# Nine expert tiles placed between attention's last batch and its routing, with the weight preparation brought forward

## The reference, cut to what matters

```python
def reference(x, ctx, Wq, bq, Wk, bk, Wv, bv, Wr, W1, b1, W2, b2):
    # x (4, 512, 256), ctx (4, 512, 192), all fp32
    q = layernorm(x) @ Wq + bq                 # (4, 512, 256)
    k, v = ctx @ Wk + bk, ctx @ Wv + bv
    x = x + softmax(q @ k.T / sqrt(256)) @ v   # per batch
    z = layernorm(x)
    probs = softmax(z @ Wr.T)                  # 8 experts
    top_v, top_i = top_k(probs, 2)
    top_v = top_v / sum(top_v)
    for e in range(8):                         # W1 (8, 1024, 256), W2 (8, 256, 1024)
        h = gelu(z @ W1[e].T + b1[e])          # exact gelu
        x = x + (h @ W2[e].T + b2[e]) * weight_of_expert(e)
    return x
```

## Time and profile before

| | us |
|---|---|
| median of three runs | 446.9 (446.31 to 447.02) |
| the profiled execution | 444.12 |
| its span, first to last instruction | 442.1 |
| first softmax of batches 0, 1, 2, 3 (ACT) | 37.49, 70.67, 110.05, 151.77 |
| first matmul of tile 0 (PE) | 214.57 |
| POOL's last scatter | 434.06 |
| PE busy over the span | 364.9 (83%) |
| DVE, ACT, POOL busy | 272.9, 234.2, 147.2 |

### The profile page before, as it was taken

How to read it: one execution, slowest core, us unless ns; L and a number is a source line. 1 busy time by engine, 2 the same in 40 slices (tenths; PEclk the granted TensorE clock), 3 DMA queues, 4 the chain that set the end, 5 groups by cost and what they waited for, 6 DMA issues and landing times. The chain is left out here.

```text
span 442.1 us, 10231 instructions
## 1 busy us (share of the span) xinstructions
PE 364.9 (83%) x3384; PEld 289.9 (66%) x3384; DVE 272.9 (62%) x764; ACT 234.2 (53%) x459; POOL 147.2 (33%) x129
## 2 busy tenths in 40 slices
PE   3999989968879795410479999999999999999980
PEld 0344645544646374410469999999999999999970
DVE  1202776687585958688056677776677776677760
ACT  0224668485655665533326656656656666666530
POOL 7300301033536470857003333333333333333331
PEclk9999999999997998655689999999999999999995
DMA  6920025611944292512423335343333333432222
GB/s 214 318 102 0 2 95 192 218 56 49 305 170 131 55 279 101 194 55 84 131 52 49 50 51 51 55 57 51 54 53 56 52 50 49 52 50 38 27 26 24
DMA packets 51794, 40.85 MB, mean 92 GB/s; under 512 B 29440, under 2 KB 47488, under 8 KB 51616
## 3 DMA queue, kind: packets, MB, share of 16 engines
q1 hardware_dynamic: 40416, 26.31, 22.6%
q0 software_dynamic: 7584, 10.57, 13.8%
q10 hardware_dynamic: 3744, 3.31, 2.2%
HBM read 22.41 MB, written 12.66 MB: 79 GB/s over the span
## 5 line engine op out<-in xcount | busy, mean ns | idle before, releaser
L444 POOL DMA_INDIRECT out<-y,meta x39 | 67.7, 1736 | 158.8 <-DVE y L1220 148.2
L855 ACT ACTIVATE g<-s_ps,b_sb,down 128x128 f32<-128x128 f32 x156 | 63.1, 454 | 57.7 <-PE s_ps L650 57.6
L664 PE MATMUL o_ps<-w2h,gh 128*128 x312 | 85.5, 274 | 4.6 <-DVE gl L1191 4.5
L664 PE MATMUL o_ps<-w2l,gh 128*128 x312 | 85.5, 274 | 0.0
L664 PE MATMUL o_ps<-w2h,gl 128*128 x312 | 85.5, 274 | 0.0
L855 ACT ACTIVATE g<-t_ps,b_sb,down 128x128 f32<-128x128 f32 x156 | 63.0, 454 | 40.2 <-PE t_ps L650 40.2
L1189 DVE TENSOR_SCALAR gh<-g,up 128x512 f16<-128x512 f32 x78 | 38.0, 487 | 68.5 <-ACT g L855 54.4
L650 PE MATMUL s_ps<-xs,w1h 128*128 128x128 f16 x624 | 61.4, 222 | 20.5 <-DMA xs<-rows 20.5
L650 PEld LDWEIGHTS s_ps<-xs,w1h 128*128 x624 | 48.6, 99 | 24.0 <-DMA xs<-rows 20.6
L650 PE MATMUL t_ps<-xs,w1h 128*128 128x128 f16 x624 | 60.5, 220 | 0.0
L1191 DVE SCALAR_TENSOR_TENSOR gl<-g,up,gh 128x512 f16<-128x512 f32 x78 | 58.6, 752 | 2.8
(11 more groups left out here) (149 smaller groups left out, 566.8 us busy)
## 6 DMA issues: line engine op xcount, KB each, us to landing
staged<-W1T SPq DMA_DIRECT2D x8, 1024.0 KB, 5.7
staged<-W2T SPq DMA_DIRECT2D x8, 1024.0 KB, 6.0
out<-x_sb ACTq DMA_DIRECT2D x4, 512.0 KB, 7.0
rows<-send POOLq DMA_DIRECT2D x8, 130.0 KB, 7.2
w2l<-ctxT SPq DMA_DIRECT2D x4, 256.0 KB, 4.4
x_sb<-x SPq DMA_DIRECT2D x2, 512.0 KB, 9.0
x_sb<-x ACTq DMA_DIRECT2D x2, 512.0 KB, 5.7
b_sb<-b SPq DMA_DIRECT2D x1, 1024.0 KB, 5.0
```

Of the source, the lines that this page charges most:

```text
L444: pool.indirect_dma_start(out=out, out_offset=bass.IndirectOffsetOnAxis(ap=meta[:, t % XR, 3:4].bitcast(I32), axis=0), in_=y2[:, t % 2, :] ...
L664: i = nc.tensor.matmul(y_ps[t % 2][:, 0:D], l[:, t % 2, m, :], second_weight(w, m, e), start=(m == 0 and k == 0), stop=(m == MC - 1 and k ...
L855: i = nc.scalar.activation(g[:, t % 2, m, :], h_ps[s][:, (m % MQ) * TR:(m % MQ + 1) * TR], ACT.Gelu, bias=b1_sb[:, bass.ds(e, 1), m:m + 1] ...
```

## The change

Nine tiles are taken from batches 0 and 1 alone: full tiles of 128 rows, of which 1024 tokens times 2 give at least nine whatever the routing. Their table (`early_tables`) is worked out by DVE in the last batch, from the row counts after batch 1. SP loads their rows when the sends of batches 0 and 1 are in, and PE starts them right after the last `attend`. The last batch's norm, transpose, logits, routing and sends now stand between these tiles' steps on each engine; three further pieces (`late_tables_1` to `_3`) make the table of the other 30 tiles.

For PE to start there, all 16 units must be prepared by then (`low_ready` 16). So the preparation is regrouped by expert, with one sum and one `scale` for two units: three experts in each of batches 0 and 1 (`SUM_A`, `SUM_B`, `SUM_C`), two in batch 2. The ring still has three slots and the same wait. `XR` goes from 8 to 6, the gated result `y2` has four buffers (`YR`), the gate is multiplied on ACT (`weigh`) and not on DVE, and b2 is loaded after six tiles' rows and not after two. Buffers that were in SBUF only after attention now stand beside it.

```diff
+EARLY = 9
-XR = 8
+XR = 6
+YR = 4
+SUM_A = {0: 0, 1: 3, 2: 6}
+SUM_B = {0: 1, 1: 4}
+SUM_C = {0: 2, 1: 5, 2: 7}
...
@@ sync: the loads of units keep their wait; the contexts move
             for u in range(RING, UNITS):
-                if u % QT == 1 and u // QT + 1 < B:
-                    load_ctx(u // QT + 1)
+                if u == 7:
+                    load_ctx(2)
+                if u == 13:
+                    load_ctx(3)
                 load_unit(u)
...
+            sp.wait_ge(tables_ready, 1)
+            for i in range(2):
+                sp.wait_ge(sent[i], 32 * QT)
+            sp.wait_ge(proj_full, uses["q", B - 1, DC - 1] + 1)
+            for t in range(XR):
                 load_rows(t)
+            sp.wait_ge(low_ready, UNITS - RING + 1)
             sp.dma_start(b2_sb[:], b2.partition_broadcast(P)).then_inc(b2_in, 16)
+            for t in range(XR, EARLY):
+                load_rows(t)
+            sp.wait_ge(tables_ready, 2)
+            for i in range(2):
+                sp.wait_ge(sent[i], 16 * NT)
+            for t in range(EARLY, TILES):
                 load_rows(t)
...
@@ gpsimd: the last batch's sends stand behind the first scatters
             for t in range(TILES):
+                if t == EARLY:
+                    pool.wait_ge(stored, 16 * B)
                 scatter(t)
+                if t < 2:
+                    send_rows(B - 1, t)
...
@@ tensor: in the tile loop
                     hidden(t, m, e_of[t])
+                if (t, m) == (1, 5):
+                    turn_normal(B - 1)
+                if (t, m) == (2, 1):
+                    logits(B - 1)
+                if (t, m) == (3, 2):
+                    ranks(B - 1)
...
@@ scalar: in the loop over batches
+            squares(0)
             for b in range(B):
...
-                if b:
-                    high(u - 1)
-                square(u)
-                if b and b + 1 < B:
+                if last:
+                    high(UNITS - 1)
+                highs(SUM_A, b)
+                if b and not last:
                     load_x(b + 1)
...
+                if b in SUM_B:
+                    squares(SUM_B[b])
+                elif not last:
+                    square(2 * SUM_C[b])
+                if not last:
+                    keys(b + 1)
+                take_turned(b, 3)
+                if not last:
+                    highs(SUM_B, b)
                     turned_rows("xt", b + 1)
+                    if b in SUM_B:
+                        squares(SUM_C[b])
                     values(b + 1)
+                    if b not in SUM_B:
+                        square(2 * SUM_C[b] + 1)
                     queries(b + 1)
                     rows_hi(b)
+                    if b + 1 in SUM_A:
+                        highs(SUM_C, b)
+                        squares(SUM_A[b + 1])
+                    else:
+                        high(2 * SUM_C[b])
...
@@ vector: in the loop over batches
                 row_max(b, 0)
                 if b >= 2:
                     route_places(b - 2)
                 row_max(b, 1)
                 if b:
+                    lows(SUM_C, b - 1)
+                scale(SUM_A, b)
                 row_max(b, 2)
                 invert(b, 0)
                 if b:
                     route_logits(b - 1)
+                ln1_moments(b + 1)
                 residual(b, 0)
                 row_max(b, 3)
                 invert(b, 1)
+                keys(b + 1)
+                ln1_apply(b + 1)
+                lows(SUM_A, b)
                 residual(b, 1)
                 ...
                 values(b + 1, (0, 1))
                 aggregate(1, b, stats2_ready, ln2_var)
+                lows(SUM_B, b)
                 values(b + 1, (2, 3))
                 ...
+                scale(SUM_C, b)
```

More of the change, by code:

```diff
@@ L146, in build, with again_as @@
-        b1q = sa("b1q", [P, E, MC])
-        x_sb = sa("x_sb", [P, 2, QT, D])
+        taken_early = sb("taken_early", [P, E])
+        meta = sb("meta", [P, XR, ROW - D])
+        gates = sb("gates", [P, YR, 3])
+        def again_as(early, late):
+            with ExitStack() as held:
+                first = [sb(*a, scope=held) for a in early]
+            return first, [sb(*a) for a in late]
+        (wq_sb, wk_sb, wv_sb), (xs,) = again_as(
+            [("wq_sb", [P, DC, D]), ("wk_sb", [P, 2, D]), ("wv_sb", [P, 2, D])],
+            [("xs", [P, XR, 2, DC, TR], F16)])
@@ new lines, in _ @@
+            n_late = TILES - EARLY
+            late = slice(EARLY, TILES)
+            by_expert = late_space[:, 0:6 * E].rearrange("p (k e) -> p k e", e=E)
+            by_tile = late_space[:, 6 * E:6 * E + 7 * n_late].rearrange("p (k t) -> p k t", t=n_late)
+            below = late_space[:, LK:LK + E * (N // TR)].rearrange("p (e t) -> p e t", t=N // TR)
+            tile_expert = late_space_2[:, 0:2 * n_late * E].rearrange("p (k t e) -> p k t e", k=2, e=E)
+            count, rest, tiles, last, first, shift = (by_expert[:, k, :] for k in range(6))
@@ new lines, in _, with per_tile, per_expert, late_tables_1 @@
+            ended, mine, less_tile, first_tile, offset, start, region = (by_tile[:, k, :] for k in range(7))
+            product, belongs = tile_expert[:, 0], tile_expert[:, 1]
+            def per_tile(a):
+                return a.unsqueeze(2).to_broadcast([P, n_late, E])
+            def per_expert(a):
+                return a.unsqueeze(1).to_broadcast([P, n_late, E])
+            def late_tables_1():
+                link(nc.vector.tensor_tensor(count, nextrow[:, B, :], base[:], ALU.subtract))
+                link(nc.vector.scalar_tensor_tensor(out=rest, in0=taken_early[:], scalar=-float(TR), in1=count,
+                                                    op0=ALU.mult, op1=ALU.add))
+                link(nc.vector.tensor_tensor(below, rest.unsqueeze(2).to_broadcast([P, E, N // TR]),
+                                             steps[:].unsqueeze(1).to_broadcast([P, E, N // TR]), ALU.is_gt))
+                link(nc.vector.tensor_reduce(tiles, below, AX.X, ALU.add))
+                link(nc.vector.tensor_tensor_scan(last, tiles, none[:], 0.0, ALU.add, ALU.add))
+                link(nc.vector.tensor_tensor(first, last, tiles, ALU.subtract))
+                link(nc.vector.tensor_tensor(shift, first, taken_early[:], ALU.subtract))
@@ L1058, in _, with lows @@
+            def lows(hook, b):
+                if b in hook:
+                    low(2 * hook[b])
+                    low(2 * hook[b] + 1)
             ln1_moments(0)
@@ L1064, in _ @@
             queries(0)
[L1065 to L1066 removed]
+            for b in range(B - 1):
                 row_max(b, 0)
@@ L1122, in _ @@
-            route_first(B - 1)
-            route_second(B - 1)
-            route_gates(B - 1)
-            route_places(B - 1)
-            low(UNITS - 3)
-            low(UNITS - 2)
-            scale(UNITS - 1)
-            dve.wait_ge(gate_ready, B)
-            def per_tile(a):
-                return a.unsqueeze(2).to_broadcast([P, TILES, E])
-            def per_expert(a):
-                return a.unsqueeze(1).to_broadcast([P, TILES, E])
-            count, tiles, last, first = (by_expert[:, k, :] for k in range(4))
@@ L1140, in _ @@
-            ended, mine, less_tile, first_tile, offset, start, region = (by_tile[:, k, :] for k in range(7))
-            product, belongs = tile_expert[:, 0], tile_expert[:, 1]
-            link(nc.vector.tensor_tensor(count, nextrow[:, B, :], base[:], ALU.subtract))
-            link(nc.vector.tensor_tensor(below, count.unsqueeze(2).to_broadcast([P, E, N // TR]),
-                                         steps[:].unsqueeze(1).to_broadcast([P, E, N // TR]), ALU.is_gt))
-            link(nc.vector.tensor_reduce(tiles, below, AX.X, ALU.add))
```

478 lines of the change are left out of this document (256 added, 222 removed).

## The result

After: median **466.41 us** (463.52 to 469.22, four runs). Before, in the same comparison: 446.61 us (441.12 to 447.02, four runs). The ratio is 1.0473 with a 95% interval of 1.0357 to 1.0588: slower, by 4.7%. The forecast was 468 us. The profiled execution took 464.15 us with a span of 462.3, where the sum had 463.0.

A forecast was written before the change was run, and what follows sets the result against it. PE bounds the tiles, not the 39.4 us stretch ahead that the change fills; longer attention puts tile 0 at 230.6, plus tiles 219.5 and tail 12.9 gives 463.0, plus 4.8 gives 467.8, said as 468 us; range 450 to 487.

The forecast's parts named there:

- the sum: Whole kernel: tile 0 at 230.6, tiles 219.5, tail 12.9 give a span of 463.0 us; 4.8 more gives 467.8.
- The ring: Attention, batches 0 and 1: six second squares wait for low, then load, then square, 9.9 us each; 51 us added.
- The three steps between: Attention, first softmaxes of batches 1, 2, 3: 27.3 us later, 30.1 us more, then 6.0 us less.
- The first rival: Attention: ring waits don't add up, only ACT's added 9.8 us counts; tile 0 near 187, 424 us; chance 0.09.
- The fit that the prediction quotes: Load landings: 2.0 us plus bytes at 436 GB/s, 4.4 us for 1 MB; forecast 460; the sum used 5.7.
- The clock: PE in attention: low level 0.50 after the new waits costs 0 to 12 us, taken as 4.
- The second rival: Attention: PE stays at 0.50 through batches 0 and 1, work behind waits counts double; 480 to 492 us; chance 0.16.
- The last stretch: Softmax 3 to attention's end: kept at 23.4 us as before, so attention ends at 226.6.
- The wait for x: Batch 1: x's store, issued behind the late softmax, holds batch 2's load of x; 7.0 + 5.7 = 12.7 us.
- The tiles: Tile 0 to PE's end: 206.7 + 5 + 3.3 + 1 + 3.5 = 219.5 us, against 214.6 before.
- PE's wait for the routing choice: Early tiles: PE waits about 5 us before its ranks, because b2's late arrival holds DVE's result 0.
- The loads of tiles 8 and 9: Rows behind scatters and sends: in time by about 1 us, 0 to 5 us taken as 0; rival of starving, chance 0.10.

## Why the prediction was right

It was right in direction and size, and the waits at the ring are there as forecast. But it put all that attention grows down to the ring, which is 35 us of 57; and its sum for the tiles was right while one of its parts was missing.

- **The ring.** Forecast: six waits of 5 to 10 us at the squares of units 3 to 13, softmaxes at 98.0, 167.5 and 203.2. Measured: 5.22 to 9.21 us, softmaxes at 101.33, 171.29 and 208.76. The three steps between were 27.3, 30.1 and -6.0 us; they were 30.7, 30.6 and -4.2. Leaving out the loads and adding a slot each bring softmax 3 back by 35 us, so this is shown and not only read from the order. The first rival (waits that don't add up) asked for less than 30 us in all; there were 40.4, and the chain runs through them. The six landings in the chain took 5.3 to 6.2 us, near the 5.7 of the sum. The fit that the prediction quotes from the Trainium skill ("DMA: Bandwidth & Descriptors", Anatomy of one DMA) is given there for DMAs that GpSimd issues; these loads are SP's.
- **What the ring is not.** The sum calls 51 us what the ring adds. The walk through the orders that gave them had ACT's two highs and squares in it as well, so the time came out; the name was wrong. Without any wait for a load softmax 3 is still 21.8 us later than before, and tile 0 is at 196.3 and 196.7 in the two kernels, not near the 187 that the first rival gave for ACT's added work alone.
- **The clock.** I took 4 us, after softmax 3. The low level is there (0.71 and 0.67), and may be part of the 5.6 us by which softmax 3 comes later than the steps without it. The second rival (480 us and more) asked for it throughout; the queries were slow, but the eight scores of the next batch, of the same shape, were not (3.69 us in the chain, at 87.14, where eight such matmuls have 3.67 in the earlier trace rows). The gap ahead of the low level in the earlier trace rows, which the prediction sets beside waits for DMA, was a wait of 2.33 us for ACT.
- **The last stretch.** I kept 23.4 us from softmax 3 to attention's end; it was 18.0. This balances the 5.6 us above, so that attention's end at 226.75 (forecast 226.6) is better than its parts: luck. That tile 0's rows land at the same time held (226.72). Up to tile 0 the stretch is 19.3 us here and 21.5 to 23.1 in the eight kernels of the experiments up to the changed kernel without sends; DVE's pause of 2.7 to 4.4 us beside batch 1's sends, which they have and this profile has not, fits the difference.
- **The wait for x.** 12.7 us of store and load were counted in batch 1. The load landed in 3.5 us and nothing in that batch waits for it, so this part was wrong. Batch 1 was as long as forecast all the same (70.0 against 69.5), which is luck; what stands in its place, perhaps the low clock (0.67 there), was not taken apart.
- **The tiles.** Forecast 219.5, measured 221.06. PE's wait for the routing choice was 5.74 (5 taken); but of the reason given, b2's arrival, it holds only some 2.1. The other 3.6 are the chain of logits and choice itself, and stay with b2 in time. The loads of tiles 8 and 9 were in time, as taken: no wait for rows.
- **What was missing.** The sends' hold on PE was in no step. In the changed kernel all that the sends cost is 3 to 5 us by the comparison without them, whose intervals overlap, and its profile has no burst; in the kernels whose tiles start 32 us earlier it is 13, and eats what the shorter attention gives. Had I forecast those, I would have been wrong by that much. The sends of batches 2 and 3 were in the kernel before too, but there they stood in PE's empty stretch, so its profile could not show the price: they were moved beside the work that they hold up.

## What to carry to other kernels

When work is pulled ahead through a small ring on engines that go in order, follow the order by hand: a square that stands behind a load that stands behind a low costs their sum each time, whatever the busy shares say, and one more slot removes the wait. It does not remove the work that was brought forward: here 35 us went and 22 stayed. When a stretch that looked empty is filled, ask what else ran in it: DMA issues that cost nothing beside an idle engine can cost a working one. After a wait has gone, measure the end and not the place: here 31 us came back as 20, until the sends were spaced.

## What the runs showed of the hardware

Indirect row sends issued by GpSimd eight in a row, or four and four (0.96 us each, 1.27 us apart), hold up other engines' instructions. PE comes in bursts 0.7 us apart with no semaphore to wait for (eight matmuls in 4 us instead of about fifty), and is then granted 0.50 for 7 to 14 us. The tiles take 231 to 235 us in the five kernels that have them in both batches and meet the bursts, 220.9 with the sends spaced, and 218.3 without; the profiled run of the changed kernel, at 221.06, has them and escaped. b2's transfer is not needed for it, nor a busy DMA (share 0.30 in the worst stretch). What in the chip is held (the fetching of instructions, a queue, descriptors being written) no run here tells. "Runtime: NRT & Kernel Launch", Instruction fetch mechanics, in the Trainium skill says that each engine's sequencer fetches its own instructions by DMA in blocks and that this is mostly hidden. The traces list packets of a kind `instruction`, of 16 or 8 KB, and the bursts do not follow their arrival: with four slots none moves between 202.5 and 214 us, while PE's bursts run from 204.6 to 211.8. In the changed kernel with b2 first, bursts run from 267.7 to 277.9; the DMA list from 272 to 279 names two kinds and not this one:

```profile
q0 software_dynamic: 315, 0.65, 36.8%
q1 hardware_dynamic: 688, 0.13, 11.9%
```

So PE goes on by small steps with no block arriving; what it waits for in each step stays open.
